# Laying out a softmax buffer query by query instead of head by head, in a fused cross-attention and mixture-of-experts kernel

## The chip, the cores and the metric

The kernel runs on one core of a Trainium2 chip. The metric is the device time of one execution in microseconds, the median of several runs. One core has five engines with queues of their own: TensorE (PE, matrix products, with its weight loads shown as PEld), VectorE (DVE), ScalarE (ACT), GpSimd (POOL) and SyncE (SP, here only DMA). They order each other by semaphores.

## The reference

A batch of 16 sequences of 256 tokens (width 128) attends to a context of 64 tokens for each sequence, with 16 heads of 8 dimensions. The softmax is taken over the heads, not over the keys. A mixture of experts follows (2 shared experts, 8 routed ones of which each token takes 2).

```python
q, k, v = (heads of x Wq, ctx Wk, ctx Wv)               # [b, h, s, 8]
scores = einsum('bhqd,bhkd->bhqk', q, k) / sqrt(8)
attn = softmax(scores, axis=1)                          # axis 1 is the head
x = einsum('bhqk,bhkd->bhqd', attn, v); out = x Wo
x = x + out;  x = x + layernorm(x) + shared_out + routed_out
```

## The kernel before

The kernel has a preparation (weights split into high and low fp16 parts, projections of queries, keys and values), the attention stage, the shared experts and the routed experts. The change lies wholly in the attention stage.

Two sequences make a pair: 8 pairs. The 128 partitions of a tile hold the 2 x 64 keys of a pair, and the free axis holds heads and queries. A unit is one pair and 128 of its queries for each sequence; there are 16 units (u), taken four at a time (k = 0 to 3), and a buffer `E` (L110) has a slot for each of the four: 16 heads x 128 queries of fp32 for each partition, 8 KB a slot. Before the change a head's 128 queries are adjacent, and the heads of one query are 512 bytes apart.

A unit passes through the engines in this order:

- TensorE, `raw_scores` (L1247): 16 products of 128 columns into `scores`, four PSUM banks (L185). There is one such set, so the raw scores of a unit wait for the exponentials of the unit before (`exp_done`).
- VectorE, `max_heads` (L850): the maximum over heads, read from PSUM.
- TensorE, `minus_max` (L1256): four products that subtract the maximum in PSUM.
- ScalarE, `exps` (L575): two instructions of 8 heads each, from PSUM to E.
- VectorE, `sum_heads` (L855): the sum over the 16 heads of each query, read from E; then the reciprocal (L858) into `rZ`.
- GpSimd, `normalise` (L377): E times `rZ` in place, two instructions of 8 heads.
- TensorE, `weighted_values` (L1263): 16 fp32 products. The padded values `vPad` are the stationary operand; 128 columns of E, one head, are the moving one.
- ScalarE, `copy_o` (L568), TensorE, `project_out` (L1274), VectorE, `add_attention` (L862): the output projection, added to X.

The order on the queues is written out by hand in the functions `four_units`. On TensorE (L1282) unit u issues its raw scores, the output projection of unit u - 3, the first half of the values of unit u - 2, `minus_max` of u, and the second half of the values of u - 2; in some units transposes for the experts follow (`ffn_transposes`, L1313). On VectorE (L865) unit u issues its maximum, the sum and reciprocal of unit u - 1, `add_attention` of u - 3, and in two of four units the statistics of a layer norm (L826, L831, L840 to L845). ScalarE's `four_units` (L609) puts the exponentials first, and behind them the copy of the output, the padding of keys and values (`pad_k` L518, `spread_v` L528) and the parts of the second layer norm (L589 to L607). GpSimd's (L404) has the normalisation, some small steps of the layer norm (L390) and a difference (L401).

Later stages use the same memory under other names, through the flat view `E_flat` (L145), which is the same bytes before and after the change. The routing of tokens (`choose`, L957 to L974, and `place`, L991 to L1000) has small VectorE instructions on tables of 8 experts by tiles: L974 writes the bf16 table `member` with the experts of a token 32 elements of 2 bytes apart, L960 has the same shape and writes adjacent words, L996 reads 4-byte words 128 bytes apart, and L1014 writes one 4-byte word in each row of 516 bytes.

Of the kernel before, what the change touches and what calls it, by code (L numbers as in the profile page):

```python
# [29 lines left out]
ACT = mybir.ActivationFunctionType  # L30
AX_X = mybir.AxisListType.X

P = 128
D = 128
B, S, SK = 16, 256, 64
H, DK = 16, 8
HH = H // 2
# [28 lines left out]
def xattn_moe_kernel(nc, x, ctx_t, wq_t, wk_t, wv_t, wo_t, cent_t, rbias, wfc_t, wproj_t, out, gathered, results):  # L66
    with ExitStack() as stack:
        def sb(name, shape, dt=F32):
            return stack.enter_context(nc.sbuf_tensor(name, shape, dt))
# [37 lines left out]
        Mx = sb("Mx", [P, 2, P], BF16)  # L107
        Z = sb("Z", [P, 2, P])
        rZ = sb("rZ", [P, 2, P])
        E = sb("E", [P, 4, H, P])  # L110
        oT = sb("oT", [P, 2, 2, P])
        x2 = sb("x2", [P, 2, TILES * P], F16)
        wfcH = sb("wfcH", [P, NE, F], F16)
# [28 lines left out]

        yk = q_flat.bitcast(F32).rearrange("p (a k t d) -> p a k t d", a=PAIRS, k=2, t=TP)
        yg = vPad[0][:].rearrange("p a s -> p (a s)")[:, 0:NG * 2 * D].rearrange("p (k s d) -> p k s d", k=NG, s=2)
        E_flat = E[:].rearrange("p a h q -> p (a h q)")  # L145

        wfc_f32 = E_flat[:, 0:NE * F].rearrange("p (e f) -> p e f", e=NE)
        NR = 12
# [36 lines left out]
        scores = banks[:, 0:4, :]  # L185
# [124 lines left out]
        def _(pool):  # L310
            g = nc.gpsimd
# [61 lines left out]
            def normalise(k, u):  # L373
                pool.wait_ge(rz_ready, u + 1)
                for half in range(2):
                    heads = E[:, k, half * HH:half * HH + HH]
                    g.tensor_tensor(heads, heads, rZ[:, k % 2, :].unsqueeze(1).broadcast_to([P, HH, P]),  # L377
                                    ALU.mult).then_inc(attn_ready, 1)

            def inverse_deviation(n):  # L380
# [23 lines left out]
            def four_units(n):  # L404
                normalise(0, 4 * n)
                if n > 1:
                    ffn_inputs(2 * n - 3, 1)
                normalise(1, 4 * n + 1)
                if n:
                    inverse_deviation(n - 1)  # L410
                normalise(2, 4 * n + 2)
                normalise(3, 4 * n + 3)
                if 0 < n < PAIRS // 2 - 1:
                    ffn_inputs(2 * n - 2, 0)
# [54 lines left out]
        def _(act):  # L469
            s = nc.scalar  # L470
# [99 lines left out]
            def exps(u, k, again):  # L570
                act.wait_ge(s_ready, u + 1)
                if again:
                    act.wait_ge(o_ready, u - 3)
                for i in range(2):
                    s.activation(E[:, k, 8 * i:8 * i + 8], scores[:, 2 * i:2 * i + 2], ACT.Exp,  # L575
                                 scale=DK ** -0.5).then_inc(exp_done, 1)

            act.wait_ge(wfcL_ready, NE)
# [30 lines left out]
            def four_units(n, first=False, second=False, third=False, last=False):  # L609
                for k in range(4):  # L610
                    u = 4 * n + k
                    exps(u, k, not first)
                    if not (first and k < 2):
                        if not first:
                            act.wait_ge(y_ready, u - 3)
                        copy_o(u - 2, k)
                    if k == 0 and not (first or second):
                        second_norm(n - 2, 1, not third)
                    if k == 0 and not first:
                        pad_k(1, 2 * n + 1)  # L620
                    if k == 1 and not first:
                        spread_v(1, 2 * n + 1)
                    if k in (1, 2) and not (first or second):
                        add_norm(n - 2, k - 1)
                        copy_x2(2 * n - 5 + k)
                    if k == 2 and not last:
                        pad_k(0, 2 * n + 2)
                    if k == 3 and not last:
                        spread_v(0, 2 * n + 2)
                if not first:  # L630
                    second_norm(n - 1, 0, not second)
# [80 lines left out]
        def _(dve):  # L712
            v = nc.vector
# [138 lines left out]

            def sum_heads(u, k):
                dve.wait_ge(exp_done, 2 * u + 2)
                v.tensor_reduce(Z[:, k % 2, :], E[:, k].rearrange("p h q -> p q h"), AX_X,  # L855
                                ALU.add).then_inc(z_ready, 1)
                dve.wait_ge(z_ready, u + 1)
                v.reciprocal(rZ[:, k % 2, :], Z[:, k % 2, :]).then_inc(rz_ready, 1)  # L858
# [6 lines left out]
            def four_units(n, first, second):  # L865
                for k in range(4):
                    u = 4 * n + k
                    max_heads(u, k)
                    if not (first and k == 0):
                        if not (first and k < 3):  # L870
                            dve.wait_ge(attn_ready, 2 * u - 4)
                        sum_heads(u - 1, (k - 1) % 4)
                    if not (first and k < 3):

                        add_attention(u - 3, (k + 1) % 2, 2 * n + (k - 3) // 2)
                    if k in (1, 2) and not first:
                        pair_stats(n - 1, k - 1)
                    if k == 2 and not first:
                        deviation_seed(n - 1, not second)
# [3 lines left out]
            with dve.Fori(2, PAIRS // 2) as n:  # L883
                four_units(n, False, False)
            dve.wait_ge(attn_ready, 2 * UNITS - 4)
            sum_heads(UNITS - 1, 3)
            dve.wait_ge(small_loaded, 32)
            v.tensor_copy(centH[:], cent[:]).then_inc(rstep, 1)
# [261 lines left out]
            for k in range(REST):  # L1150
                i = NG * ROUNDS + k
# [21 lines left out]
        def _(pe):  # L1173
# [7 lines left out]
            for i in range(2):  # L1181
                for p in range(4):
                    last = t.matmul(v_ps[i][:, D * p:D * p + D], ctxT[:, 4 * i + p].rearrange("p b s -> p (b s)"), wv,
                                    start=True, stop=True)
# [75 lines left out]
            def weighted_values(u, k, half):  # L1260
                pe.wait_ge(attn_ready, 2 * u + half + 1)
                for h in range(HH):
                    last = t.matmul(o_ps[:, P * half:P * half + P], vPad[k // 2][:, half, h * P:(h + 1) * P],  # L1263
                                    E[:, k, half * HH + h, :], start=(h == 0), stop=(h == HH - 1))
                if half:
                    last.then_inc(o_ready, 1)

# [14 lines left out]
            def four_units(n, first=False, inputs=False):  # L1282
                for k in range(4):
                    u = 4 * n + k
                    if k % 2 == 0:
                        pe.wait_ge(kPad_ready, 2 * n + k // 2 + 1)
                    raw_scores(u, k, 2 * n + k // 2, first and k == 0)
                    if not (first and k < 3):
                        project_out(u - 3, (k - 3) % 4, first and k == 3)
                    values = not (first and k < 2)  # L1290
                    if values:
                        if k % 2 == 0:
                            pe.wait_ge(vPad_ready, 2 * n + k // 2)
                        if first and k == 3:
                            pe.wait_ge(oT_ready, 1)
                        weighted_values(u - 2, (k - 2) % 4, 0)
                    minus_max(u, k)
                    if values:
                        weighted_values(u - 2, (k - 2) % 4, 1)
                    if k in (1, 2) and inputs:  # L1300
                        ffn_transposes(2 * n - 5 + k, n > 2 or k > 1)
# [22 lines left out]
            for half in range(2):  # L1324
                weighted_values(UNITS - 2, 2, half)
# [154 lines left out]
            for k in range(REST):  # L1480
                i = NG * ROUNDS + k
# [37 lines left out]
```

## Time and profile before

| | us |
|---|---|
| median of 3 runs | 599.83 |
| lowest and highest run | 597.85, 602.25 |
| span of the profiled execution, from its first to its last instruction | 516.6 |
| attention stage, from the first unit's scores to the last values | about 76 to 222 in that span |

The span is what the trace covers; the device time has a further 83 us around it. The page lists each engine's busy time and the costliest groups of instructions. Busy shares of the whole span are means over stages with different limits, so the attention stage is read by itself, in stretches of four units.

### The profile page before, as it was taken

To read this page: it belongs to the slowest core of one execution; us is meant where nothing else is said; L and a number is where in the kernel's file an instruction comes from. 1 tells how busy PE (TensorE), PEld (TensorE's weight loads), DVE (VectorE), ACT (ScalarE), POOL (GpSimd) and SP (SyncE) were. 2 spreads that over 40 slices of the span, in tenths; PEclk is the share of its full clock that TensorE was granted. 3 is DMA by queue.
4 is the path that set the end of the run, shared out by engine and by line. 5 is a ranking of instruction groups with operands and counts; after the bars stand their busy time and mean duration, and the time that the engine had idled before them with its cause. 6 is when DMAs were issued, how large, how long until landed. Compare 5 with 4: busy or idle time off the path is not lost.

```text
span 516.6 us, 11703 instructions
## 1 busy us (share of the span) xinstructions
PE 383.5 (74%) x3844; PEld 306.4 (59%) x3845; DVE 368.1 (71%) x663; ACT 291.5 (56%) x525; POOL 278.2 (54%) x276
## 2 busy tenths in 40 slices
PE   5457754988688698685899879949979797979600
PEld 2223322877577687583566557637969696869500
DVE  4947775889999999969948786734747464646437
ACT  3764423434567575534678568925746464646446
POOL 7392001664576667650776777631757475656700
PEclk9967885889999899797899899987999898999955
DMA  8900000000000000000111123122322222221089
GB/s 228 394 14 2 0 0 0 1 1 1 1 1 1 0 2 1 0 1 2 42 52 39 52 82 104 32 58 58 87 63 81 71 63 68 66 75 53 23 213 275
DMA packets 36234, 29.82 MB, mean 58 GB/s; under 512 B 4181, under 2 KB 33496, under 8 KB 35809
## 3 DMA queue, kind: packets, MB, share of 16 engines
q1 hardware_dynamic: 31648, 20.84, 14.0%
q0 software_dynamic: 4544, 8.44, 5.0%
q8 instruction: 26, 0.43, 0.3%
q14 instruction: 16, 0.12, 0.1%
HBM read 17.55 MB, written 12.62 MB: 58 GB/s over the span
## 4 chain that ended last, share of the span: by engine, by line
PE 29%; DVE 7%; issue 7%; POOL 3%; DMA 2%; ACT 1%; SPq 1%; POOLq 0%; DVEq 0%
PE banks L1440 3%; PE banks L1455 3%; PE banks L1441 3%; PE banks L1442 3%; PE banks L1454 3%; PE banks L1456 3%; POOL results L456 2%; PE banks L1422 2%; DVE E L919 2%; PE banks L1372 2%; PE banks L1376 1%; PE banks L1374 1%; PE banks L1356 1%; PE banks L1357 1%; PE banks L1358 1%
## 5 line engine op out<-in xcount | busy, mean ns | idle before, releaser
L377 POOL TENSOR_TENSOR E<-E,rZ 128x1024 f32<-128x1024 f32 x32 | 75.2, 2371 | 89.5 <-DVE rZ L858 89.5
L456 POOL DMA_INDIRECT results<-vPad,qRep x78 | 84.8, 1087 | 65.8 <-DVE vPad L1127 43.0
L446 POOL DMA_INDIRECT gathered<-xs,slot x64 | 69.5, 1085 | 42.5 <-DVE xs L1000 18.9
L1135 DVE TENSOR_TENSOR E<-kRep,E 128x512 f16<-128x512 f32 x78 | 54.2, 694 | 41.9 <-ACT E L689 41.9
L687 ACT ACTIVATE kRep<-banks 128x512 f32<-128x512 f32 x78 | 46.8, 600 | 64.8 <-PE banks L1442 48.8
L1263 PE MATMUL banks<-E,vPad 128*128 128x128 f32 x512 | 70.1, 296 | 12.5 <-POOL E L377 12.5
L1263 PEld LDWEIGHTS banks<-E,vPad 128*128 128x128 f32 x512 | 67.5, 210 | 17.1 <-issue 8.8
L575 ACT ACTIVATE E<-banks 128x1024 f32<-128x1024 f32 x32 | 31.0, 1021 | 57.3 <-PE banks L1256 57.3
L855 DVE TENSOR_REDUCE Z<-E 128x128 f32<-128x2048 f32 x16 | 59.3, 3706 | 0.0
L1454 PE MATMUL banks<-wprojL,E 128*128 x312 | 57.5, 223 | 0.9 <-DVE E L1135 0.9
L919 DVE TENSOR_TENSOR E<-kRep,E 128x512 f16<-128x512 f32 x64 | 45.9, 732 | 16.1 <-ACT E L650 15.5
L1455 PE MATMUL banks<-wprojH,E 128*128 x312 | 57.2, 223 | 0.0
L1456 PE MATMUL banks<-wprojH,E 128*128 x312 | 57.1, 223 | 0.0
L1372 PE MATMUL banks<-wprojL,E 128*128 128x128 f16 x256 | 48.6, 226 | 11.4 <-DVE E L919 11.2
L649 ACT ACTIVATE kRep<-banks 128x512 f32<-128x512 f32 x64 | 38.7, 605 | 27.6 <-PE banks L1358 25.4
L1374 PE MATMUL banks<-wprojH,E 128*128 128x128 f16 x256 | 48.5, 226 | 0.0
L1376 PE MATMUL banks<-wprojH,E 128*128 128x128 f16 x256 | 48.5, 226 | 0.0
L689 ACT ACTIVATE E<-banks 128x512 f16<-128x512 f32 x78 | 47.0, 602 | 0.0
L850 DVE TENSOR_REDUCE Mx<-banks 128x128 bf16<-128x2048 f32 x16 | 36.5, 2280 | 13.3 <-PE banks L1247 13.2
L1440 PE MATMUL banks<-qRep,wfcH 128*128 128x256 f16 x156 | 44.6, 286 | 0.0
L1442 PE MATMUL banks<-qRep,wfcH 128*128 128x256 f16 x156 | 44.5, 285 | 0.0
L1441 PE MATMUL banks<-qRep,wfcL 128*128 128x256 f16 x156 | 44.5, 285 | 0.0
(203 smaller groups left out, 931.0 us busy)
## 6 DMA issues: line engine op xcount, KB each, us to landing
qRep<-gathered SPq DMA_DIRECT2D x39, 129.0 KB, 2.2
qRep<-results SPq DMA_DIRECT2D x16, 256.0 KB, 5.2
E<-in_wfc_t SPq DMA_DIRECT2D x1, 2560.0 KB, 9.5
X<-in_x SPq DMA_DIRECT2D x4, 512.0 KB, 7.2
out<-X SPq DMA_DIRECT2D x8, 256.0 KB, 3.9
xs<-in_wproj_t SPq DMA_DIRECT2D x1, 1280.0 KB, 12.2
results<-vPad,qRep POOLq DMA_INDIRECT x78, 2.5
gathered<-kPad SPq DMA_DIRECT2D x9, 129.0 KB
```

What stands on the lines that cost most here:

```text
L377: g.tensor_tensor(heads, heads, rZ[:, k % 2, :].unsqueeze(1).broadcast_to([P, HH, P]), ALU.mult).then_inc(attn_ready, 1)
L446: g.indirect_dma_start(out=gathered, out_offset=bass.IndirectOffsetOnAxis(ap=slot[:, k, i:i + 1], axis=0), in_=xs[:, i, :], in_offset=None ...
L456: g.indirect_dma_start(out=results, out_offset=bass.IndirectOffsetOnAxis(ap=xg[:, k, h, 2 * D:ROW].bitcast(I32), axis=0), in_=yg[:, k, h, ...
L855: v.tensor_reduce(Z[:, k % 2, :], E[:, k].rearrange("p h q -> p q h"), AX_X, ALU.add).then_inc(z_ready, 1)
L1263: last = t.matmul(o_ps[:, P * half:P * half + P], vPad[k // 2][:, half, h * P:(h + 1) * P], E[:, k, half * HH + h, :], start=(h == 0), sto ...
L1372: t.matmul(o, hidH[:, e, c, tok], wprojL[:, e, f], start=(e == 0 and c == 0 and q == 0), stop=False, skip_group_check=True)
L1440: t.matmul(o, wfcH[:, e, f], xgT[:, j, 1], start=True, stop=False)
L1441: t.matmul(o, wfcL[:, e, f], xgT[:, j, 0], start=False, stop=False)
L1442: last = t.matmul(o, wfcH[:, e, f], xgT[:, j, 0], start=False, stop=True)
L1454: t.matmul(o, gH[:, j, c, tok], wprojL[:, e, f], start=(c == 0), stop=False)
L1455: t.matmul(o, gH[:, j, c, tok], wprojH[:, e, f], start=False, stop=False)
L1456: last = t.matmul(o, gL[:, j, c, tok], wprojH[:, e, f], start=False, stop=(c == FC - 1))
```

## The change

The buffer E has the axis of queries outside and the axis of heads inside: the 16 heads of one query are adjacent (64 bytes), and consecutive queries of one head are 64 bytes apart. The four places that read or write E in this stage get the matching access patterns. The number of instructions, their element counts, the waits and the queues' orders stay as they are.

```diff
-        E = sb("E", [P, 4, H, P])
+        E = sb("E", [P, 4, P, H])
-        E_flat = E[:].rearrange("p a h q -> p (a h q)")
+        E_flat = E[:].rearrange("p a q h -> p (a q h)")
             def normalise(k, u):
                 for half in range(2):
-                    heads = E[:, k, half * HH:half * HH + HH]
-                    g.tensor_tensor(heads, heads, rZ[:, k % 2, :].unsqueeze(1).broadcast_to([P, HH, P]),
+                    heads = E[:, k, :, half * HH:half * HH + HH]
+                    g.tensor_tensor(heads, heads, rZ[:, k % 2, :].unsqueeze(2).broadcast_to([P, P, HH]),
                                     ALU.mult).then_inc(attn_ready, 1)
                 for i in range(2):
-                    s.activation(E[:, k, 8 * i:8 * i + 8], scores[:, 2 * i:2 * i + 2], ACT.Exp,
+                    s.activation(E[:, k, :, HH * i:HH * i + HH].rearrange("p q h -> p h q"),
+                                 scores[:, 2 * i:2 * i + 2].rearrange("p b (h q) -> p (b h) q", q=P), ACT.Exp,
                                  scale=DK ** -0.5).then_inc(exp_done, 1)
-                v.tensor_reduce(Z[:, k % 2, :], E[:, k].rearrange("p h q -> p q h"), AX_X,
+                v.tensor_reduce(Z[:, k % 2, :], E[:, k], AX_X,
                                 ALU.add).then_inc(z_ready, 1)
                     last = t.matmul(o_ps[:, P * half:P * half + P], vPad[k // 2][:, half, h * P:(h + 1) * P],
-                                    E[:, k, half * HH + h, :], start=(h == 0), stop=(h == HH - 1))
+                                    E[:, k, :, half * HH + h], start=(h == 0), stop=(h == HH - 1))
```

## Rows read from the trace of the kernel before

**Rows 1.** The page's busy time: us, share of the span, instructions of each engine.
```profile
PE 383.5 (74%) x3844; PEld 306.4 (59%) x3845; DVE 368.1 (71%) x663; ACT 291.5 (56%) x525; POOL 278.2 (54%) x276
```

**Rows 2.** The view of line L855, the sum over heads: durations and starts.
```profile
L855 DVE TENSOR_REDUCE Z<-E x16: 3614/3718/3756, 84.3 to 213.0; 128x128 f32<-128x2048 f32 x16
```

**Rows 3.** Four-unit stretches: length, busy PE, PEld, DVE, ACT, POOL, PE clock, DMA.
```profile
135.55:170.80 35.25, 27.65 (x256) 24.79 (x256) 33.78 (x38) 24.85 (x44) 23.69 (x24) 1.00 0.00 1
170.80:205.97 35.17, 29.18 (x256) 26.01 (x256) 33.81 (x39) 22.26 (x40) 23.67 (x24) 0.95 0.00 1
```

**Rows 4.** Groups by line, 120 to 220 us: busy us, mean ns, idle before.
```profile
L377 POOL TENSOR_TENSOR E<-E,rZ 128x1024 f32<-128x1024 f32 x23 | 53.8, 2358 | 32.4 <-DVE rZ L858 32.4
...
L855 DVE TENSOR_REDUCE Z<-E 128x128 f32<-128x2048 f32 x12 | 44.6, 3718 | 0.0
L850 DVE TENSOR_REDUCE Mx<-banks 128x128 bf16<-128x2048 f32 x10 | 22.8, 2276 | 1.5 <-PE banks L1247 1.4
L575 ACT ACTIVATE E<-banks 128x1024 f32<-128x1024 f32 x22 | 21.3, 1020 | 35.2 <-PE banks L1256 35.2
```

**Rows 5.** Timeline, 140 to 158 us: start, duration, engine, line.
```profile
147.95 1.94 ACT L575 ACTIVATE E<-banks 128x1024 f32<-128x1024 f32 x2 [3.92 <-PE banks L1256]
...
149.54 1.06 PE L1247 MATMUL banks<-qRep,kPad 128*128 128x128 f16 x16
149.62 4.67 POOL L377 TENSOR_TENSOR E<-E,rZ 128x1024 f32<-128x1024 f32 x2 [2.41 <-DVE rZ L858]
...
150.43 1.11 PE L1274 MATMUL banks<-wo,oT 128*128 128x128 f32 x8
150.63 2.29 DVE L850 TENSOR_REDUCE Mx<-banks 128x128 bf16<-128x2048 f32 x1 [0.81 <-PE banks L1247]
...
152.03 2.05 PE L1263 MATMUL banks<-E,vPad 128*128 128x128 f32 x16 [0.49 <-POOL E L377]
...
152.84 3.75 DVE L855 TENSOR_REDUCE Z<-E 128x128 f32<-128x2048 f32 x1
...
153.92 1.03 PE L1256 MATMUL banks<-Mx,negI 128*128 128x512 bf16 x4
...
154.78 1.95 PE L1263 MATMUL banks<-E,vPad 128*128 128x128 f32 x16
...
156.63 0.95 DVE L858 RECIPROCAL rZ<-Z 128x128 f32<-128x128 f32 x1
```

**Rows 6.** Small VectorE instructions, by line and shape (L1014: its line's own view).
```profile
L974 DVE TENSOR_TENSOR member<-E 128x192 bf16<-128x192 f32 x1 | 1.0, 992 | 0.0
L974 DVE TENSOR_TENSOR member<-E 128x64 bf16<-128x64 f32 x1 | 0.4, 439 | 0.0
L960 DVE TENSOR_TENSOR E<-E,kPad 128x192 f32<-128x192 f32 x2 | 0.7, 357 | 0.1
L960 DVE TENSOR_TENSOR E<-E,kPad 128x64 f32<-128x64 f32 x2 | 0.4, 224 | 0.1
L996 DVE TENSOR_TENSOR E<-E 128x192 f32<-128x192 f32 x2 | 1.0, 480 | 0.0
L996 DVE TENSOR_TENSOR E<-E 128x64 f32<-128x64 f32 x2 | 0.5, 258 | 0.0
L959 DVE TENSOR_REDUCE kPad<-E 128x24 f32<-128x192 f32 x2 | 0.7, 352 | 0.1
L959 DVE TENSOR_REDUCE kPad<-E 128x8 f32<-128x64 f32 x2 | 0.4, 220 | 0.1
L1014 DVE COPY xs<-token x2: 160/177/194, 280.1 to 329.3; 128x24 int32<-128x24 int32 x1, 128x8 int32<-128x8 int32 x1
```

**Rows 7.** ScalarE instructions of other sizes and patterns, by line and shape.
```profile
L655 ACT ACTIVATE E<-E 128x384 f32<-128x384 f32 x1 | 0.5, 523 | 3.4 <-DVE E L941 3.4
L655 ACT ACTIVATE E<-E 128x128 f32<-128x128 f32 x1 | 0.3, 310 | 0.0
L528 ACT ACTIVATE vPad<-V 64x128 f32<-64x128 f32 x16 | 4.9, 303 | 0.1
```

**Rows 8.** Other GpSimd products of two tensors, by line and shape.
```profile
L362 POOL TENSOR_TENSOR wfcH<-E,consts 128x512 f32 x10 | 10.0, 1042 | 9.2 <-DMA E<-in_wfc_t 9.2
L423 POOL TENSOR_TENSOR X<-X,xn 128x512 f32<-128x512 f32 x4 | 5.4, 1387 | 0.0
```

## The prediction

> **What bounds the kernel now.** I read the page's busy table first: no engine is above 74% of the span [rows 1], so the question is which stretch the change touches and what ends last there. The buffer E holds exponentials only in the attention stage, 16 units that run from about 76 to 222 us. The row of the sum over heads gives the period: 16 sums start from 84.3 to 213.0 us, so one unit takes 128.7 / 15 = 8.58 us [rows 2]. The table by stretch takes four units at a time, from one maximum over heads to the fourth after it. VectorE is busy 33.8 of 35.2 us, TensorE 27.7 and 29.2, ScalarE 24.9 and 22.3, GpSimd 23.7 [rows 3]. VectorE is the bound of this stage. Its costliest group is the sum over heads at L855, 3.72 us each, followed by the maximum at L850 with 2.28 [rows 4].
>
> The timeline of one unit shows the second constraint, a ring of waits [rows 5]. One set of four PSUM banks holds the scores, so the next raw scores can't start before the exponentials of this unit are read out. On TensorE's queue the order is: raw scores (1.06 us), output projection of three units ago (1.11), first half of the values of two units ago (2.05), subtraction of the maximum (1.03), second half of the values (1.95), next raw scores. The exponentials (1.94 for both halves) start after the subtraction. The ring is therefore: exponentials 1.94, the second half of the raw scores 0.53 (its first half needs only the first exponentials), projection 1.11, values 2.05, subtraction 1.03, and about 0.4 for handoffs, 7.1 us, below VectorE's 8.58. It has about 1.5 us of slack. The second ring runs over two units: sum, reciprocal (0.95), the first half of the normalisation on GpSimd (half of 4.67), values, subtraction, exponentials, raw scores, maximum, next sum: 3.75 + 0.95 + 2.34 + 2.05 + 1.03 + 1.94 + 1.06 + 2.29 = 15.4, with handoffs near 16.4, or 8.2 us for each unit [rows 5].
>
> **The change, part by part.** It adds and removes no instruction, wait or DMA. It changes the order of addresses in four kinds of instructions, all in this stage.
>
> *Sum over heads (VectorE, 16).* Its innermost read goes from a step of 512 bytes to adjacent words. Now it costs 3718 ns for 2048 elements, 1.8 ns each [rows 4]. Small reductions over 8 adjacent words take 352 ns for 192 elements and 220 for 64 [rows 6]: (352 - 220) / 128 = 1.03 ns each, and 154 ns fixed. So 2048 x 1.03 + 154 = 2.27 us, a gain of 1.45 us in each unit. The maximum over heads, the same count read from PSUM, takes 2.28 [rows 4]. This part I take as firm. The gain is 1.45 x 16 = 23 us of VectorE work if nothing else ends later.
>
> *Exponentials (ScalarE, 32).* They read the same scores and now write single 4-byte words 64 bytes apart. Before: 1020 ns for 1024 elements [rows 4]; between two ScalarE rows of 128 and 384 elements (310 and 523 ns [rows 7]) one element costs 0.83 ns, which leaves 0.17 us fixed. No ScalarE row in this trace writes single words apart; the nearest writes 8-word runs (L528, 303 ns for 128, no dearer than adjacent ones [rows 7]). So I bound it. Below: no added cost, 1.94 us for both halves. Above: the row with exactly this step is on VectorE. L974 writes 2-byte elements 64 bytes apart at (992 - 439) / 128 = 4.3 ns each, while L960, the same shape with adjacent writes, costs (357 - 224) / 128 = 1.04 [rows 6]. Between them stands L1014, 4-byte words 516 bytes apart: (194 - 160) / 16 = 2.1 ns each [rows 6]. The new write shares its step with L974 and its word size with L1014. Neither row is clearly the nearer, so I take a value between them, 2.7 ns: 2 x (0.17 + 1.024 x 2.7) = 5.9 us for a unit against 1.94. At 4.3 ns it is 9.1.
>
> The Trainium skill has a measurement of its own for this ("Vector Engine (DVE) Microarchitecture Reference", section 5.2): on VectorE a port keeps its full rate only over pairs of adjacent words, and a destination that steps 24 words each element runs at 2.50 ns. By that figure, as an estimate, a unit's exponentials would take 5.5 us and the forecast would be about 6 us lower. The trace agrees with the direction (1.04 against 4.3 ns in the rows just named); no run here shows ScalarE under it.
>
> *Weighted values (TensorE, 512 records, 32 for each unit).* E is the operand that streams past the weights; each column of 128 partitions was the neighbour of the last and is now 64 bytes away. Sixteen records take 1.95 us now, 122 ns each [rows 5]. No TensorE row in the trace streams with such a step. Below: no added cost. Above: VectorE reads 4-byte words 128 bytes apart (L996) at (480 - 258) / 128 = 1.73 ns, and 512 bytes apart at 1.8 ns [rows 4, 6]. If a hop costs that whichever engine reads, 128 columns take 230 ns and a half of the values 16 x 0.23 = 3.7 us. If each record reads its columns twice, it is 7.4. I take 3.7, since the trace already shows each fp32 product as two records (512 for 256 products), one for each pass over the columns. This lies on both rings and fully on TensorE's queue.
>
> *Normalisation (GpSimd, 32).* It reads and writes runs of 8 words, and the reciprocal is repeated innermost. Now 2358 ns for 1024 elements, 2.3 ns each [rows 4]. GpSimd's other products of two tensors run at 1042 / 512 = 2.0 ns (with an innermost repeated operand) and 1387 / 512 = 2.7 [rows 8]. So 2.1 to 2.8 us each; I take no change. At 2.8 it adds 0.9 us to a unit of a queue that is busy 23.7 of 35.2 us [rows 3], under the slack of the sum.
>
> **The sum.** Ring over the exponentials: 5.9 + 0.53 + 1.11 + 3.7 + 1.03 + 0.4 = 12.7 us. TensorE's own queue: 1.06 + 1.11 + 3.7 + 1.03 + 3.7 + 0.3 (the transposes) = 10.9. VectorE after the gain: (33.8 - 4 x 1.45) / 4 = 7.0. The ring decides. 12.7 - 8.58 = 4.1 us for each of 15 intervals, 62 us, and about 3 us more behind the last exponentials, where the last values run alone. The profiled execution spans 516.6 us; the median of the runs shown is 599.83, 83.2 more, in which this change does nothing. So 516.6 + 65 = 582 in the profile, and 599.8 + 65 = 665 us. The 23 us saved on VectorE are not subtracted: they turn into idle time there.
>
> **The rivals.**
> *Hops are free for ScalarE and TensorE (faster).* Then VectorE's gain counts until the two-unit ring holds: (16.4 - 1.45) / 2 = 7.5 us, with some of the extra VectorE work of the fourth unit still showing, about 7.5 x 4 + 0.7 = 30.7 for four units against 35.2. That is 1.1 us each, 18 us: 582 us. For it: ScalarE and TensorE have no strided row that is slow here, and the 8-word runs of L528 cost nothing extra. Against it: every VectorE row with single words apart is dearer [rows 6]. It decides as long as the exponentials stay under 1.94 + 1.5 = 3.4 us for a unit and half of the values under about 2.7. The Trainium skill states the like for one engine ("ScalarE: Activation LUTs", the section on the stages of an ACTIVATE: one element per cycle whatever the function); it says nothing of strides, so it does not raise this chance.
> *Both hops cost what far hops cost on VectorE.* Exponentials 2 x (0.17 + 1.024 x 1.73) = 3.9, values 3.7: ring 10.7, TensorE's queue 10.9. 2.3 x 15 + 3 = 38: 638 us. If TensorE's hop is free with this, the ring is 8.9 and the time 604 to 612.
> *The 64-byte step costs ScalarE what L974 shows.* 9.1 + 6.8 = 15.9: 7.3 x 15 + 3 = 113: 713 us.
> *TensorE becomes the bound, reading each column twice.* 1.06 + 1.11 + 7.4 + 1.03 + 7.4 + 0.3 = 18.3: 9.7 x 15 + 7 = 153: 752 us. "SBUF — State Buffer" of the Trainium skill (section "Door 1", the note on cachelines) says that each access crossing into a new 16-byte line pays, and steps above 4 fp32 words are not free. That speaks for some price on this read too, without a figure.
>
> **Chances.** Free hops 0.18; write at the far-hop price, or only one of the two priced, 604 to 640, 0.26; the forecast's case, 640 to 690, 0.28; L974's price, up to 735, 0.15; TensorE at twice, 0.13. The likeliest case's own range is 635 to 690. The range that leaves out less than 2 in 10 goes from 582 to 735. About 1% is what a measurement of this kernel can tell from no change: faster 0.18, within 1% 0.06, slower 0.76.
>
> **What would show it.** L855 near 2.27 us shows the gain. L575 says which write price holds (1.0, 1.9, 2.9 or 4.6 us each). Sixteen records of L1263 in 2.0, 3.7 or 7.4 us say which read price. If my ring holds, VectorE's wait for raw scores before L850 grows from 1.4 us in ten units [rows 4] to several us in each unit, and the maximum is followed by idle time, not by work. The forecast is wrong if L575 stays near 1.0 us; if it is right and TensorE has no gap in this stage, then the reads and not the writes set the time.

## The result and the profile after

| | before, us | changed, us | ratio (95% interval) |
|---|---|---|---|
| first comparison, 4 runs each | 598.96 | 616.83 | 1.0285 (1.0238 to 1.0331) |
| comparison again on another chip (13 and 4 runs) | 513.49 | 529.34 | 1.0307 (1.0267 to 1.0348) |

The changed kernel is 17.9 us slower, 3%. The forecast was 665 us: the sign was right, the size nearly four times too large (65 us against 17.9).

The kernel before takes 513 us on some chips and 592 to 600 on others; the trace of before, with its span of 516.6 us, fits the first kind, and the changed kernel's first trace (span 615.6) the second. The prediction took the 83 us between the span and the median for time around the program. That was wrong. In the changed kernel the span is within 2 us of the device time. Between its two traces, of 615.6 and 527.8 us, about 60 of the 88 us lie in the stage of the shared experts (TensorE has one gap of 18.7 us there, from 338.5 to 357.2) and nearly all the rest in the routed experts, which this change does not touch. So the traces of before and after are compared in the attention stage alone, and the experiments go by their own kernel before, run on the same chip. That stage is a little longer than the 76 to 222 us given above: in the trace of before the first raw scores start at 72.0, and the last unit's products with E, behind the first routing products, end at 231.0.

The view of the changed kernel's groups by line, 120 to 220 us (busy us, mean ns, idle before and who ended it), answers to [rows 4]:

```profile
L1264 PE MATMUL banks<-E,vPad 128*128 128x128 f32 x323 | 73.8, 394 | 0.0
...
L377 POOL TENSOR_TENSOR E<-E,rZ 128x1024 f32<-128x1024 f32 x21 | 40.9, 1970 | 46.8 <-DVE rZ L859 46.8
L575 ACT ACTIVATE E<-banks 128x1024 f32<-128x1024 f32 x21 | 38.8, 1949 | 25.4 <-PE banks L1257 25.4
L851 DVE TENSOR_REDUCE Mx<-banks 128x128 bf16<-128x2048 f32 x10 | 22.9, 2291 | 29.1 <-PE banks L1248 29.0
L856 DVE TENSOR_REDUCE Z<-E 128x128 f32<-128x2048 f32 x10 | 22.8, 2276 | 0.0
```

The sum over heads fell from 3718 to 2276 ns, as forecast. The exponentials rose from 1020 to 1949 ns and the products from 291 to 394 ns a record (these durations overlap; what a record costs its queue is read from the timeline below). The maximum over heads now waits 29.0 us for raw scores in ten units, against 1.4 before: VectorE has gone from the bound to waiting. GpSimd's normalisation became cheaper, 1970 against 2358 ns, which was not forecast.

The view by stretch of the changed kernel (length; busy PE, PEld, DVE, ACT, POOL; clock) answers to [rows 3]:

```profile
142.00:180.00 38.00, 38.00 (x243) 34.26 (x242) 26.32 (x36) 28.26 (x39) 19.69 (x20) 1.00 0.00 1
180.00:218.00 38.00, 38.00 (x238) 34.38 (x236) 25.93 (x34) 30.15 (x42) 19.18 (x24) 1.00 0.00 1
```

TensorE is busy 38.00 of 38.00 us. The timeline of one unit shows what fills it:

```profile
159.08 1.09 PE L1248 MATMUL banks<-qRep,kPad 128*128 128x128 f16 x16
...
160.00 1.11 PE L1275 MATMUL banks<-wo,oT 128*128 128x128 f32 x8
160.20 2.29 DVE L851 TENSOR_REDUCE Mx<-banks 128x128 bf16<-128x2048 f32 x1 [3.94 <-PE banks L1248]
160.95 3.65 PE L1264 MATMUL banks<-E,vPad 128*128 128x128 f32 x16
...
164.43 1.04 PE L1257 MATMUL banks<-Mx,negI 128*128 128x512 bf16 x4
...
165.30 3.65 PE L1264 MATMUL banks<-E,vPad 128*128 128x128 f32 x16
165.50 3.69 ACT L575 ACTIVATE E<-banks 128x1024 f32<-128x1024 f32 x2 [0.76 <-PE banks L1257]
...
168.77 0.62 PE L1314 MATMUL banks<-ident,xs 128*128 128x128 f16 x8
```

Sixteen records take 3.65 us, 228 ns each; before they took 1.95 to 2.05 [rows 5]. From raw scores at 159.08 to the transposes at 168.77 there is no gap, 9.69 us of TensorE's queue. This is the prediction's own sign that the reads and not the writes set the time: L575 dearer, and TensorE without a gap. The line of the sum gives the mean period:

```profile
L856 DVE TENSOR_REDUCE Z<-E x16: 2274/2276/2286, 86.4 to 229.1; 128x128 f32<-128x2048 f32 x16
```

(229.1 - 86.4) / 15 = 9.51 us, against 8.58 [rows 2]. That is 0.93 x 15 = 14.0 us. The first sum also comes later: 14.05 us after the first raw scores against 12.37, since the first exponentials take 3.59 us against 1.94. Together 15.7 us, against 15.9 and 17.9 measured. This leaves out what comes behind the last sum: the last product with E starts 20.4 us after it, against 17.7 before. But in the run with the sum alone changed, which has neither hop, that is 20.3 us too, so this part can't be put down to the hops.

### The profile page after: what moved, and what is told of

It is laid out like the page before. It is cut to its first block, busy times and chain, and to the rows that moved or that the text cites. A ratio compares the mean times of both kernels' runs of the same rounds, so it can differ in the third digit from the quotient of the medians.

```text
span 615.6 us, 11703 instructions
## 1 busy us (share of the span) xinstructions
PE 453.6 (74%) x3844; PEld 355.7 (58%) x3845; DVE 345.1 (56%) x663; ACT 318.0 (52%) x525; POOL 259.0 (42%) x276
## 4 chain that ended last, share of the span: by engine, by line
PE 60%; DVE 12%; issue 10%; another core or an unknown queue 7%; ACT 5%; DMA 3%; POOL 1%; SPq 1%; DVEq 1%; ACTq 0%; POOLq 0%
PE banks L1264 18%; PE banks L1443 4%; PE banks L1456 3%; PE banks L1455 3%; PE banks L1257 3%; PE banks L1457 2%; PE banks L1441 2%; PE banks L1275 2%; PE banks L1442 2%; PE banks L1248 2%; PE banks L1373 2%; PE banks L1377 2%; PE banks L1359 2%; PE banks L1358 2%
## 5 line engine op out<-in xcount | busy, mean ns | idle before, releaser
L1264 PE MATMUL banks<-E,vPad 128*128 128x128 f32 x512 | 116.6, 394 | 0.0
L377 POOL TENSOR_TENSOR E<-E,rZ 128x1024 f32<-128x1024 f32 x32 | 62.7, 1982 | 116.1 <-DVE rZ L859 116.1
L446 POOL DMA_INDIRECT gathered<-xs,slot x64 | 64.9, 1013 | 107.3 <-DVE xs L1015 58.0
L1264 PEld LDWEIGHTS banks<-E,vPad 128*128 128x128 f32 x512 | 104.1, 211 | 6.8
L575 ACT ACTIVATE E<-banks 128x1024 f32<-128x1024 f32 x32 | 58.7, 1939 | 48.5 <-PE banks L1257 48.5
L1373 PE MATMUL banks<-wprojL,E 128*128 128x128 f16 x256 | 52.4, 235 | 33.1 <-DVE E L920 27.8
L1455 PE MATMUL banks<-wprojL,E 128*128 x312 | 63.6, 231 | 7.9 <-DVE E L1136 7.7
L1456 PE MATMUL banks<-wprojH,E 128*128 x312 | 62.8, 231 | 1.8 <-issue 1.8
L1457 PE MATMUL banks<-wprojH,E 128*128 x312 | 62.8, 231 | 1.1 <-issue 1.1
L1377 PE MATMUL banks<-wprojH,E 128*128 128x128 f16 x256 | 52.1, 234 | 11.0 <-issue 11.0
L1373 PEld LDWEIGHTS banks<-wprojL,E 128*128 128x128 f16 x256 | 26.8, 105 | 52.1 <-DVE E L920 34.3
L1375 PE MATMUL banks<-wprojH,E 128*128 128x128 f16 x256 | 52.4, 235 | 2.7 <-issue 2.7
## 6 DMA issues: line engine op xcount, KB each, us to landing
X<-in_x SPq DMA_DIRECT2D x4, 512.0 KB, 6.5
```

The lines of the kernel that those rows point to most:

```text
L377: g.tensor_tensor(heads, heads, rZ[:, k % 2, :].unsqueeze(2).broadcast_to([P, P, HH]), ALU.mult).then_inc(attn_ready, 1)
L446: g.indirect_dma_start(out=gathered, out_offset=bass.IndirectOffsetOnAxis(ap=slot[:, k, i:i + 1], axis=0), in_=xs[:, i, :], in_offset=None ...
L575: s.activation(E[:, k, :, HH * i:HH * i + HH].rearrange("p q h -> p h q"), scores[:, 2 * i:2 * i + 2].rearrange("p b (h q) -> p (b h) q", ...
L1373: t.matmul(o, hidH[:, e, c, tok], wprojL[:, e, f], start=(e == 0 and c == 0 and q == 0), stop=False, skip_group_check=True)
L1377: last_product = t.matmul(o, hidL[:, e, c, tok], wprojH[:, e, f], start=False, stop=(e == 1 and c == FC - 1), skip_group_check=True)
L1455: t.matmul(o, gH[:, j, c, tok], wprojL[:, e, f], start=(c == 0), stop=False)
```

## The experiments

Theory A: the read hop (64 bytes between the columns that stream into TensorE) fills TensorE's queue, and that sets the changed kernel's time. Theory B: the write hop of the exponentials sets it, over the ring of one set of score banks, as the forecast's sum had it. The expectations in us were written against 599.8 for the kernel before; these chips run it in 513, so differences and ratios are what is compared.

The four first kernels keep the buffer's declaration of before and add one view, `Eq = E_flat.rearrange("p (a q h) -> p a q h", a=4, q=P)`.

**The sum alone.**

```diff
-                v.tensor_reduce(Z[:, k % 2, :], E[:, k].rearrange("p h q -> p q h"), AX_X,
+                v.tensor_reduce(Z[:, k % 2, :], Eq[:, k], AX_X,
```

> The kernel before, with the sum over heads alone reading adjacent words; exponentials, normalisation and products keep the old layout. So the sum adds 16 neighbouring queries of a head instead of 16 heads of a query: it is here for its time. Theory A (TensorE's queue, lengthened by the read hop, sets the time of the changed kernel): L855's sum falls from 3.72 to 2.28 us and, with nothing else dearer, the unit shrinks from 8.58 to about 7.5 us: 580 to 586 us, ratio 0.97. Theory B (the write hop of the exponentials sets it): the same number here. If instead the gain does not come out (ratio above 0.99), the two-unit ring and not VectorE bound the kernel before.

Measured: 500.32 us against 513.04, ratio 0.9735 (0.9691 to 0.9778), 12.7 us faster. Its line:

```profile
L856 DVE TENSOR_REDUCE Z<-E x16: 2268/2276/2277, 82.0 to 196.5; 128x128 f32<-128x2048 f32 x16
```

The unit takes (196.5 - 82.0) / 15 = 7.63 us. The forecast's rival of free hops had (16.4 - 1.45) / 2 = 7.5. So the gain is real and reaches the kernel's time when nothing else becomes dearer: VectorE bounds the kernel before. Of the 1.45 us, 0.95 comes out. Who waited for whom, 90 to 196 us (us in total, times, longest), for VectorE and for TensorE:

```profile
DVE Mx L851 <- PE banks L1248: 11.9, 9, 3.3
...
PE banks L1257 <- DVE Mx L851: 7.9, 3, 2.6
PE banks L1264 <- POOL E L378: 4.3, 7, 0.9
```

The mean hides unlike units. From sum to sum, four units in a row take 6.27, 7.77, 10.29 and 7.74 us; the long one has VectorE's layer norm work in it, and the short one is about what TensorE's queue takes by its starts with cheap reads, 9.69 - 2 x 1.7 = 6.3. The ring's 7.5 is near the mean, but TensorE waited for the normalisation only 4.3 us in all, so this trace doesn't show that ring as the bound.

**The write alone.**

```diff
-                    s.activation(E[:, k, 8 * i:8 * i + 8], scores[:, 2 * i:2 * i + 2], ACT.Exp,
+                    s.activation(Eq[:, k, :, HH * i:HH * i + HH].rearrange("p q h -> p h q"),
+                                 scores[:, 2 * i:2 * i + 2].rearrange("p b (h q) -> p (b h) q", q=P), ACT.Exp,
```

> The kernel before, with the exponentials alone written 64 bytes apart; the readers keep the old layout, so they take heads and queries mixed up: it is here for its time. Both theories: 1.94 us for one exponential instruction. Theory A: the ring over the exponentials grows from 7.1 to 8.8 us, about VectorE's own 8.6: 600 to 608 us. Theory B: the write carries most of the loss, 612 us or more.

Measured: 524.51 us, ratio 1.0206 (1.0147 to 1.0265), 11.5 us slower. The exponentials, 120 to 200 us:

```profile
L576 ACT ACTIVATE E<-banks 128x1024 f32<-128x1024 f32 x18 | 32.9, 1930 | 17.7 <-PE banks L1258 17.7
```

This is more than theory A's 0 to 8 us and reaches to theory B's 12. The unit takes (222.2 - 86.9) / 15 = 9.02 us. Who TensorE waited for, 90 to 222 us:

```profile
PE banks L1249 <- ACT E L576: 18.2, 22, 2.1
PE banks L1258 <- DVE Mx L852: 7.9, 3, 2.6
PE banks L1265 <- POOL E L378: 3.2, 7, 0.6
```

The ring over the exponentials now holds: raw scores wait for them in 22 places. A's figure had this ring, but not that every fourth unit takes 11.8 us here, with the dear sum and the layer norm on VectorE, while most others take 8.0 to 8.8. The two-unit ring gives (16.4 + 1.74) / 2 = 9.07 us, near the mean, but the waits are not on it. By itself, with the old sum in place, the write hop costs two thirds of what the whole change costs.

**The read alone**, with the normalisation, which must match it:

```diff
-                    heads = E[:, k, half * HH:half * HH + HH]
-                    g.tensor_tensor(heads, heads, rZ[:, k % 2, :].unsqueeze(1).broadcast_to([P, HH, P]),
+                    heads = Eq[:, k, :, half * HH:half * HH + HH]
+                    g.tensor_tensor(heads, heads, rZ[:, k % 2, :].unsqueeze(2).broadcast_to([P, P, HH]),
-                                    E[:, k, half * HH + h, :], start=(h == 0), stop=(h == HH - 1))
+                                    Eq[:, k, :, half * HH + h], start=(h == 0), stop=(h == HH - 1))
```

> The kernel before, with the weighted values reading columns 64 bytes apart and the normalisation in the new layout (it has to go with the products); exponentials and sum keep the old one, so heads and queries are mixed up: it is here for its time. Theory A: a half of the values takes 3.65 us instead of 2.0, TensorE has no gap in the attention stage, the unit takes 9.7 us, and the time is that of the changed kernel, 613 to 620 us, though the sum still costs 3.72. Theory B: below 606 us.

Measured: 527.02 us, ratio 1.026 (1.0216 to 1.0305), 14.0 us slower. Its stretch and its sum:

```profile
120.00:200.00 80.00, 80.00 (x505) 72.41 (x505) 68.50 (x74) 45.33 (x79) 40.19 (x48) 1.00 0.00 1
...
L856 DVE TENSOR_REDUCE Z<-E x16: 3611/3769/3823, 83.7 to 225.8; 128x128 f32<-128x2048 f32 x16
```

TensorE is full, 80.00 of 80.00 us, and the unit takes 9.48 us, the changed kernel's 9.51, though here the exponentials cost 1021 ns and the sum still 3769. TensorE waits for no other engine between 95 and 226 us. With the read hop in place it makes no difference to the period whether the sum is cheap and the write dear or the other way round.

**The changed kernel without the read hop:** the edits to the sum and to the exponentials, products and normalisation as before.

> The changed kernel with products and normalisation put back to the old layout; the sum and the exponentials keep the new one, so heads and queries are mixed up: it is here for its time. Theory A: without the read hop the unit falls from 9.5 to the ring over the exponentials, 8.2 to 8.8 us: 594 to 602 us. Theory B: the write hop still sets the time, 612 to 617 us.

Measured: 511.83 us, ratio 0.9974 (0.994 to 1.0008), no difference from before that is clear of the noise, and 17 us less than the changed kernel, each beside its own kernel before. Theory B (12 us slower or more) falls. What is left is the sum's gain and the write's loss, which nearly cancel; the unit takes (212.5 - 85.8) / 15 = 8.45 us. Who TensorE waited for, 90 to 215 us:

```profile
PE banks L1249 <- ACT E L576: 19.1, 24, 2.1
PE banks L1258 <- DVE Mx L852: 5.9, 3, 2.0
```

TensorE never waits for GpSimd here, so the two-unit ring does not hold; the ring over the exponentials does. Its own length can be read from two exponentials in a row, 138.18 and 146.15 us: 7.97, where the sum of durations as in the prediction gives 3.69 + 0.53 + 1.11 + 2.05 + 1.03 + 0.4 = 8.8. With the dear reads one half of the values more, 1.7 us, would make it some 9.7 (an estimate), the same as TensorE's queue of 9.69. So in the changed kernel the queue sets the time, as the run before this one shows without the write hop, but the forecast's ring lies hardly below it.

**The changed kernel again.**

> The changed kernel as it is, once more, beside the kernel before on a chip where that takes about 513 us. If the loss belongs to the attention stage alone, the difference stays what it was, 14 to 18 us (ratio about 1.03), and the long gaps that its first trace shows in the stage of the shared experts are absent. If those gaps belonged to the change, they return and the difference grows to some 100 us.

Measured: 529.34 us against 513.49. The difference is 15.9 us, with TensorE full in the attention stage and a period of (227.8 - 84.2) / 15 = 9.57 us. The gap of 18.7 us in the stage of the shared experts is absent (no gap of TensorE there is longer than 3 us). It is not the change's.

**Pairs of queries.** If a hop is paid for each single word, two adjacent words are enough to avoid it. E is laid out as 64 pairs of queries x 16 heads x 2 queries:

```diff
+        G = 2
+        Eg = E_flat.rearrange("p (a b h g) -> p a b h g", a=4, b=P // G, h=H)
-                    heads = E[:, k, half * HH:half * HH + HH]
-                    g.tensor_tensor(heads, heads, rZ[:, k % 2, :].unsqueeze(1).broadcast_to([P, HH, P]),
+                    heads = Eg[:, k, :, half * HH:half * HH + HH]
+                    g.tensor_tensor(heads, heads, rZ[:, k % 2, :].rearrange("p (b g) -> p b g", g=G).unsqueeze(2).broadcast_to([P, P // G, HH, G]),
-                    s.activation(E[:, k, 8 * i:8 * i + 8], scores[:, 2 * i:2 * i + 2], ACT.Exp,
+                    s.activation(Eg[:, k, :, HH * i:HH * i + HH].rearrange("p b h g -> p h b g"),
+                                 scores[:, 2 * i:2 * i + 2].rearrange("p c (h b g) -> p (c h) b g", b=P // G, g=G), ACT.Exp,
-                v.tensor_reduce(Z[:, k % 2, :], E[:, k].rearrange("p h q -> p q h"), AX_X,
+                v.tensor_reduce(Z[:, k % 2, :].rearrange("p (b g) -> p b g", g=G), Eg[:, k].rearrange("p b h g -> p b g h"), AX_X,
-                                    E[:, k, half * HH + h, :], start=(h == 0), stop=(h == HH - 1))
+                                    Eg[:, k, :, half * HH + h, :], start=(h == 0), stop=(h == HH - 1))
```

> E laid out by pairs of queries: the two queries of a head are adjacent, and the pairs of the 16 heads follow each other 8 bytes apart. Exponentials and products touch runs of two words with 128 bytes between them, and the sum reads single words 8 bytes apart. If the price is one of single words (a hop is free once two adjacent words are taken), L575 is back at 1.02 us and 16 records at 2.0 us; if the sum's step of 8 bytes is as good as adjacent words, 2.28 us, the unit is the 7.6 us of the run with the sum alone changed: ratio 0.97 to 0.975. If the hop is paid by run and not by word, L575 takes about 1.5 us and the values 2.8: ratio about 1.00.

Measured: 495.53 us against 513.49, ratio 0.9605 (0.9526 to 0.9685). Its groups, 120 to 200 us:

```profile
L379 POOL TENSOR_TENSOR E<-E,rZ 128x1024 f32<-128x1024 f32 x22 | 43.3, 1987 | 23.1 <-DVE rZ L861 23.1
L1266 PE MATMUL banks<-E,vPad 128*128 128x128 f32 x321 | 42.8, 288 | 1.0 <-POOL E L379 1.0
...
L858 DVE TENSOR_REDUCE Z<-E 128x128 f32<-128x2048 f32 x10 | 22.7, 2275 | 0.6 <-ACT E L577 0.6
...
L577 ACT ACTIVATE E<-banks 128x1024 f32<-128x1024 f32 x19 | 19.0, 1053 | 17.2 <-PE banks L1259 17.2
```

The sum costs 2275 ns at steps of 8 bytes, the products 288 and the exponentials 1053 ns: all the gain and nearly nothing of the price. The unit takes (192.3 - 82.7) / 15 = 7.31 us, below the 7.63 of the run with the sum alone. GpSimd's half of the normalisation is 0.37 us shorter, and TensorE's waits for it fall from 4.3 us in seven to 1.2 in four. Over two units that would give 0.19 us for each; what makes up the rest of the 0.32 no run shows.

On a chip of the slower kind:

> The layout by pairs of queries once more, for a tighter interval. Expected 494 to 498 us where the kernel before takes 513: ratio 0.960 to 0.970.

Measured: 572.07 us against 592.42, ratio 0.9661 (0.9624 to 0.9697). This layout beats both kernels. The expected ratio held, the expected us did not, since that chip runs the kernel before in 592.

**Groups of four queries** (the same edits with `G = 4`).

> The same with groups of four queries, 16 bytes a group: exponentials and products touch runs of four words, and the sum reads single words 16 bytes apart. Exponentials 1.02 us, values 2.0 us. If the sum is only cheap while two reads in a row fall into the same 16 bytes, it is back at 3.7 us here and the ratio is 1.00; if only larger steps cost, 2.28 us and 0.97.

Measured: 512.0 us, ratio 0.9965 (0.9934 to 0.9997):

```profile
L858 DVE TENSOR_REDUCE Z<-E x16: 3785/3854/3897, 82.4 to 208.8; 128x128 f32<-128x2048 f32 x16
```

With 16 bytes from one read to the next the sum is as dear as with 512 (3854 against 3718 ns), while the exponentials (1021 ns) and the products (278 ns a record) are as cheap as in the kernel before. The gain of the sum sits wholly between steps of 8 and of 16 bytes.

**A tree of additions** in the old layout.

```diff
-                v.tensor_reduce(Z[:, k % 2, :], E[:, k].rearrange("p h q -> p q h"), AX_X,
-                                ALU.add).then_inc(z_ready, 1)
-                dve.wait_ge(z_ready, u + 1)
+                v.tensor_tensor(part[:], E[:, k, 0:8], E[:, k, 8:16], ALU.add).then_inc(z_ready, 1)
+                dve.wait_ge(z_ready, 4 * u + 1)
...
+                v.tensor_tensor(Z[:, k % 2, :], part[:, 0], part[:, 1], ALU.add).then_inc(z_ready, 1)
+                dve.wait_ge(z_ready, 4 * u + 4)
```

> The layout of the kernel before, kept for all engines, with the sum over heads made of four additions of adjacent words (1024, 512, 256 and 128 elements) into scratch memory. From the VectorE addition of 512 elements at 0.69 us: 1.22 + 0.69 + 0.42 + 0.29 = 2.6 us and some tenths of waits, against 3.72. About 1 us less for each unit: ratio 0.98. If its two read ports disturb GpSimd's normalisation (2.36 us each), part of that is lost.

Measured: 518.68 us, ratio 1.0109 (1.0072 to 1.0146), slower where 0.98 was expected. The additions on VectorE (the two last rows) run while GpSimd works:

```profile
148.30 4.66 POOL L378 TENSOR_TENSOR E<-E,rZ 128x1024 f32<-128x1024 f32 x2 [2.40 <-DVE rZ L864]
...
152.92 2.11 POOL L402 TENSOR_TENSOR xs<-xn,xs 128x512 f16<-128x512 f32 x1
...
151.14 2.90 DVE L856 TENSOR_TENSOR x<-E 128x1024 f32<-128x1024 f32 x1
154.08 1.50 DVE L858 TENSOR_TENSOR x<-x 128x512 f32<-128x512 f32 x1
```

The addition of 1024 elements takes 2.90 us here and 1.80 in the mean of 120 to 200 us, where 1.22 was worked out, and GpSimd's subtraction beside it 2.11 us, where in the changed kernel it takes 1.12. The times look like one engine standing still for the other: GpSimd's product ends at 152.96, the addition that began at 151.14 ends 1.08 us later, and the subtraction ends 0.99 us after that addition. Undisturbed, the addition takes 1.21 us and the four additions with their waits 2.72, close to what was expected; over the 16 units the four take 4.1 us in the mean, more than the 3.72 of the sum that they replace. An addition reads two operands from SBUF, a reduction one. The Trainium skill has this rule ("GPSIMD Engine Reference", Key points: GpSimd shares its SBUF interfaces with VectorE and contends with its instructions of two SBUF inputs), and this trace agrees with it.

**The price of a hop by itself:** copies of 256 elements from an adjacent source into scratch memory, at several steps.

> The kernel before with 15 small extra instructions ahead of its work, on VectorE and ScalarE, each copying 256 elements into or out of scratch memory at a given step; their durations, not the kernel's time, are what is read. Theory A (the 4.3 ns of L974 belong to its 2-byte elements): a VectorE write of 4-byte words 64 bytes apart costs about 1.7 ns an element (0.6 us for 256), the 2-byte one 4.3 (1.2 us); ScalarE's 4-byte one 1.73 (0.6 us). Theory B (they belong to the step of 64 bytes on VectorE): both VectorE writes take 1.2 us and ScalarE alone is cheaper. On steps: 8 bytes as cheap as adjacent words (0.33 us on VectorE, 0.39 on ScalarE), 16 bytes already at the full price.

The lines of the probe (min/median/max ns). VectorE, writes: adjacent, 8, 16 and 64 bytes apart, then 2-byte elements 64 bytes apart and adjacent; reads of 4-byte words 16, 8 and 32 bytes apart (L755, L757, L759). ScalarE, writes: adjacent, 8, 16, 64 bytes, then 2-byte elements 64 bytes apart and adjacent.

```profile
L741 DVE COPY qRep<-ident x1: 356/356/356, 8.1 to 8.1; 128x256 f32<-128x256 f32 x1
L743 DVE COPY qRep<-ident x1: 296/296/296, 8.4 to 8.4; 128x256 f32<-128x256 f32 x1
L745 DVE COPY qRep<-ident x1: 526/526/526, 8.8 to 8.8; 128x256 f32<-128x256 f32 x1
L747 DVE COPY qRep<-ident x1: 405/405/405, 9.3 to 9.3; 128x256 f32<-128x256 f32 x1
L749 DVE CAST qRep<-ident x1: 768/768/768, 9.8 to 9.8; 128x256 bf16<-128x256 f32 x1
L751 DVE CAST qRep<-ident x1: 293/293/293, 10.6 to 10.6; 128x256 bf16<-128x256 f32 x1
L755 DVE COPY qRep<-qRep x1: 392/392/392, 15.3 to 15.3; 128x256 f32<-128x256 f32 x1
L757 DVE COPY qRep<-qRep x1: 294/294/294, 15.7 to 15.7; 128x256 f32<-128x256 f32 x1
L759 DVE COPY qRep<-qRep x1: 389/389/389, 16.0 to 16.0; 128x256 f32<-128x256 f32 x1
L487 ACT ACTIVATE qRep<-ident x1: 409/409/409, 12.2 to 12.2; 128x256 f32<-128x256 f32 x1
L489 ACT ACTIVATE qRep<-ident x1: 432/432/432, 12.6 to 12.6; 128x256 f32<-128x256 f32 x1
L491 ACT ACTIVATE qRep<-ident x1: 661/661/661, 13.1 to 13.1; 128x256 f32<-128x256 f32 x1
L493 ACT ACTIVATE qRep<-ident x1: 640/640/640, 13.8 to 13.8; 128x256 f32<-128x256 f32 x1
L495 ACT ACTIVATE qRep<-ident x1: 1322/1322/1322, 14.4 to 14.4; 128x256 bf16<-128x256 f32 x1
L497 ACT ACTIVATE qRep<-ident x1: 418/418/418, 15.8 to 15.8; 128x256 bf16<-128x256 f32 x1
```

ScalarE's adjacent copy leaves 409 - 256 x 0.83 = 196 ns fixed. A 4-byte hop then costs (640 - 196) / 256 = 1.73 ns an element, a 2-byte one at the same 64 bytes (1322 - 196) / 256 = 4.4 ns. Adjacent 2-byte elements cost no more than adjacent words. VectorE shows the same order, 405 against 768 ns; its times are lower than expected throughout, and its adjacent copy, the first of the row, is slower than the one with a step of 8 bytes, which I can't explain. Its reads repeat the edge of the sum: 8 bytes apart 294 ns, 16 and 32 bytes apart 392 and 389. At one and the same step of 64 bytes the 2-byte element is the dear one on both engines, so theory A holds in kind; L974's 4.3 ns itself is met only on ScalarE (4.4), since VectorE's copy takes 768 / 256 = 3.0 ns at most.

## Why the prediction was wrong in size

- *The sum's gain* (1.45 us a unit): right, 3718 to 2276 ns, and in the run with this part alone it reached the kernel's time.
- *The read price* (3.7 us for half of the values): right, 3.65. So was the argument that each record passes over the columns once.
- *The write price* (2.7 ns an element, 5.9 us a unit): this step failed. It is 1.73 ns, 3.7 us a unit for both. I had taken a value between L974 and L1014 because the new write shared its step with the one and its word size with the other. The probe shows that the element size decides. The rows of 4-byte words [rows 6] had it at 1.73 to 2.1. This term put the ring at 12.7 us, above TensorE's queue of 10.9, and so named the wrong bound: 1.8 x 15 = 27 of the 48 us of error.
- *TensorE's queue* (10.9 us a unit): the right mechanism, sized too large. The forecast added durations of groups, 1.11 + 3.7 and so on. In the timeline each group starts some 0.17 us before the last one's duration ends. The starts from 159.08 to 168.77 give 9.69 where the durations add to 10.5. From sum to sum most units take 9.69, the four with transposes 10.12, the first two (less work on TensorE) 9.0 and 8.9 and the last 6.9; the mean is 9.51. 1.4 x 15 = 21 us, the rest of the error. The same addition for the kernel before gives 7.2 + 0.3, which was below VectorE's 8.58 and so did no harm there.
- *The rival "both hops cost what far hops cost"* was the true case. It gave 638 us through the same addition; with the queue read from starts it gives 617. It had been given 0.26 together with its neighbours, less than the forecast's case.
- *The two rings*: the ring over the exponentials is real, and holds in the two runs that have the write hop and the old reads; it too was sized too large by adding durations, 8.8 against 7.97 us. The two-unit ring gives 7.5 and 9.07 us where 7.63 and 9.02 were measured, but the waits in those traces lie elsewhere: its agreement with the means is luck as far as the runs show.
- *The 83 us around the span* did not enter the sum, but the statement was wrong: in every other run the span is within 2 us of the device time of the profiled execution, so the trace of 516.6 us was taken where the kernel runs in about 518 us, and the median of 599.83 elsewhere.
- *Normalisation at no change*: it became 0.39 us faster for each half, hidden behind TensorE in the changed kernel; in the layout by pairs it may be part of the gain.

## What to carry to other kernels

A layout has a writer and several readers, and a transposition moves the strided access from one engine to others; price every one, and look whether a granule of two words serves all of them. Here pairs give the sum its gain at steps of 8 bytes and leave the other engines runs of two words, 3.4 to 4% faster than before. When an engine may become the bound, its time is read from the starts of its instructions, not from the sum of their durations; and a price taken from another instruction should come from one with the same element size.

## What the runs showed of the hardware that I had not expected

- The price of single 4-byte words is nearly one figure on three engines: ScalarE's write 1.73 ns, TensorE's read 228 / 128 = 1.78 ns, the read of VectorE's sum 1.8 ns. VectorE's copies in the probe are cheaper (405 ns for 256 single words written 64 bytes apart, at most 1.6 ns each). Two adjacent words escape it on the engines tried (1053 and 288 ns against 1949 and 394 with single words).
- For VectorE's sum the edge lies between 8 bytes (2276 ns) and 16 bytes (3854 ns), and its copies (294 and 392 ns) and ScalarE's (432 and 661 ns) have it at the same place.
- A scattered 2-byte write costs ScalarE 2.5 times what a scattered 4-byte one does (4.4 against 1.73 ns).
- GpSimd's product in place got faster, 1.97 to 1.99 us against 2.36, in all three layouts in which queries are outside and heads inside. The repeated operand is innermost only in the changed kernel (1970 ns) and not in the groups of two and four (1987 and 1966 ns), so that is not the reason; which it is no run shows.
- The same program takes 513 us on two chips and 592 to 600 on others. Most of the difference shows as idle time in the stage of the shared experts; its cause was not looked for.
